# The first stage of an FFN, attention, FFN kernel: operands turned by DMA in place of TensorE

## The reference

```
x = x + 0.5 * ffn(layernorm(x))          # ffn: x and weight are quantised in blocks of 32 to a 6-bit grid
x = x + attention(layernorm(x))          #      with one scale a block, then xd @ wd.T + bias (512 x 512)
x = x + 0.5 * ffn(layernorm(x))

attention: qkv = x @ qkv_w.T + qkv_b (512 -> 1536), 16 heads of 32, each token looks at
           13 neighbouring tokens (window shifted inward at the ends of a sequence),
           softmax(q*scale . k + relative bias) . v, then @ proj_w.T + proj_b
```

## Time and profile before

| | us |
|---|---|
| median of 3 runs | 3375.26 (3371.84 to 3376.33) |
| profiled execution, its own time | 3373.88 |
| its span in the trace | 3372.0 |
| TensorE busy | 3001.5 (89%) |
| DVE busy | 2306.3 (68%) |
| ACT busy | 1888.3 (56%) |
| POOL busy | 1911.1 (57%) |

### The profile page before, as it was taken

The page is one execution under the profiler, slowest core; times in us unless marked ns, Lnnn a source line. Parts: engine busy times, 40 slices in busy tenths (PEclk is TensorE's granted clock), DMA queues, the critical chain, the costliest instruction groups (busy, mean ns, idle before and its releaser), DMA issues. The chain is left out here.

```text
span 3372.0 us, 68516 instructions
## 1 busy us (share of the span) xinstructions
PE 3001.5 (89%) x24864; PEld 1829.5 (54%) x24864; DVE 2306.3 (68%) x3170; ACT 1888.3 (56%) x2323; POOL 1911.1 (57%) x1497
## 2 busy tenths in 40 slices
PE   0399999999999999999978999999999999499999
PEld 0244444444444444444447877777777776244444
DVE  7467666666666766666556666666666665799995
ACT  2355555555555555556545666665666666566662
POOL 3354554554455455445326666666666665788883
PEclk9699999999999999999978999999999999699999
DMA  2123233323323323332247767677767674344442
GB/s 76 63 88 113 88 113 113 107 93 115 119 92 113 113 94 106 113 113 95 93 127 187 191 189 191 189 185 194 188 181 194 187 192 117 115 151 149 149 148 86
DMA packets 339610, 449.44 MB, mean 133 GB/s; under 512 B 23048, under 2 KB 254496, under 8 KB 331168
## 3 DMA queue, kind: packets, MB, share of 16 engines
q1 hardware_dynamic: 339360, 445.57, 43.4%
HBM read 243.85 MB, written 201.38 MB: 132 GB/s over the span
## 5 line engine op out<-in xcount | busy, mean ns | idle before, releaser
L761 DVE TENSOR_TENSOR fq_out_lo<-fq_val,fq_out_hi 128x512 f16<-128x512 f32 x384 | 460.7, 1237 | 289.8 <-ACT fq_out_hi L829 289.8
L946 PE MATMUL fq_acc<-fq_y_hi_t,w_qkv 128*128 128x512 f16 x2048 | 614.6, 379 | 1.6 <-ACT fq_y_hi_t L842 1.6
L1186 ACT ACTIVATE att_ctx<-att_o_ps 32x512 f32<-32x512 f32 x512 | 300.9, 588 | 365.0 <-PE att_o_ps L1295 358.7
L829 ACT CAST fq_out_hi<-fq_val 128x512 f16<-128x512 f32 x384 | 237.3, 618 | 319.1 <-DVE fq_val L758 311.0
L1270 PE MATMUL att_s_ps<-att_k,att_q_bd 128*128 128x44 f16 x6144 | 388.4, 217 | 26.2 <-DMA att_q_bd<-q_parts 16.9
L1270 PEld LDWEIGHTS att_s_ps<-att_k,att_q_bd 128*128 128x128 f16 x6144 | 382.1, 170 | 27.0 <-issue 26.0
L946 PE MATMUL fq_acc<-fq_y_lo_t,w_qkv 128*128 128x512 f16 x1024 | 388.5, 379 | 0.0
L946 PEld LDWEIGHTS fq_acc<-fq_y_hi_t,w_qkv 128*128 128x128 f16 x2048 | 200.1, 98 | 243.6 <-ACT fq_y_hi_t L842 1.8
L946 PE MATMUL fq_acc<-w_qkv,fq_y_hi_t 128*128 128x512 f16 x1024 | 304.9, 380 | 16.7 <-ACT fq_val L824 16.7
L966 PE MATMUL fq_acc<-w_ffn,fq_f_hi_t 128*128 128x512 f16 x1024 | 310.7, 386 | 1.4 <-DVE fq_f_lo_t L806 1.4
L632 PE MATMUL ffn_acc<-w_ffn,ffn_hi_t 128*128 128x512 f16 x1024 | 306.8, 381 | 4.5 <-DVE ffn_x_ring L518 4.4
(11 more groups left out here) (188 smaller groups left out, 6510.2 us busy)
## 6 DMA issues: line engine op xcount, KB each, us to landing
att_v<-v_parts SPq DMA_DIRECT2D x96, 704.0 KB
att_k<-k_parts SPq DMA_DIRECT2D x64, 524.0 KB, 7.1
fq_x<-in_L_attn_x SPq DMA_DIRECT2D x32, 1024.0 KB, 6.8
x_after_ffn<-fq_x SPq DMA_DIRECT2D x32, 1024.0 KB, 4.3
att_q_bd<-q_parts SPq DMA_DIRECT2D x512, 64.0 KB, 3.8
att_x<-x_after_ffn SPq DMA_DIRECT2D x32, 1024.0 KB, 5.9
x_after_attention<-att_x SPq DMA_DIRECT2D x32, 1024.0 KB, 9.2
ffn_x_ring<-x_after_attention SPq DMA_DIRECT2D x32, 1024.0 KB, 6.3
```

The lines of the kernel that those rows point to most:

```text
L761: dve.tensor_tensor(out=out[1][:, b], in0=val[:, b % RING], in1=out[0][:, b], op=ALU.subtract).then_inc(s["out_lo"], 1)
L829: act.copy(out[0][:, b], val[:, b % RING]).then_inc(s["out_hi"], 1)
L946: op = pe.matmul(acc[:, b % RING], w, m, start=(kc == 0 and (a, c) == (0, 0)), stop=(kc == KC - 1 and (a, c) == PARTS[-1]))
L1186: return act.activation(ctx_f[rows, u.u % 2].rearrange("p g (c q) -> p g c q", q=CHUNK), o_ps[rows, :, :, h, :], ACT.Copy, scale=1.0 / P_UP)
```

## The change

The 64 transposes that TensorE made for each group and the four copies out of PSUM are taken out. In their place SP issues four DMAs for each group (`dma_start_transpose`), from SBUF to SBUF, which write f_hi, f_lo, y_hi and y_lo transposed into `hi_t`, `lo_t`, `y_hi_t` and `y_lo_t`. Each names a source of 128x2048 fp16 and a destination of 128 x 16 x 128. `y_hi_t` and `y_lo_t` are doubled. `acc` now has all eight PSUM banks; the FFN uses banks 0 to 3, and block b of q, k and v uses bank (b + 4) % 8.

A group is now spread over four steps: t loads and takes statistics, q = t-1 is quantised, f = t-2 has its FFN and second norm, g = t-3 its q, k and v. The load of x is issued one step ahead, the store of v one step later. POOL computes the statistics of the first norm at the end of the step before the one that uses them. On DVE the value of the next v block is read before the lo part of the one at hand.

```diff
-    MID = NB - 2
+    BANKS = 8
...
-        hi, lo, hi_t, lo_t = (sb(n, [P, W], F16) for n in ("f_hi", "f_lo", "f_hi_t", "f_lo_t"))
-        y_hi, y_lo, y_hi_t, y_lo_t = (sb(n, [P, W], F16) for n in ("y_hi", "y_lo", "y_hi_t", "y_lo_t"))
+        hi, lo, y_hi, y_lo = (sb(n, [P, W], F16) for n in ("f_hi", "f_lo", "y_hi", "y_lo"))
+        hi_t, lo_t = (sb(n, [P, SUB, KC, P], F16) for n in ("f_hi_t", "f_lo_t"))
+        y_hi_t, y_lo_t = (sb(n, [P, 2, SUB, KC, P], F16) for n in ("y_hi_t", "y_lo_t"))
...
-        t_hi = ctx.enter_context(nc.psum_tensor("fq_t_hi", [P, KC, GROUP], F16))
-        t_lo = ctx.enter_context(nc.psum_tensor("fq_t_lo", [P, KC, GROUP], F16))
-        acc = ctx.enter_context(nc.psum_tensor("fq_acc", [P, RING, C], F32))
+        acc = ctx.enter_context(nc.psum_tensor("fq_acc", [P, BANKS, C], F32))
...
+                def turn_f(u):
+                    if u.within(GROUPS):
+                        need(sp, s["hi_done"], u.n + 1)
+                        take(sp, s)
+                        need(sp, s["ffn_done"], u.n * SUB)
+                        take(sp, s)
+                        sp.dma_start_transpose(hi_t[:].rearrange("p i g n -> p (i g) n"), hi[:]).then_inc(
+                            s["hi_turned"], 16)
+                        need(sp, s["lo_done"], u.n + 1)
+                        take(sp, s)
+                        sp.dma_start_transpose(lo_t[:].rearrange("p i g n -> p (i g) n"), lo[:]).then_inc(
+                            s["lo_turned"], 16)
...
+                def body(t):
+                    store_v(t.back(4))
+                    load(t.back(-1))
+                    store_x(t.back(2))
+                    turn_f(t.back(1))
+                    turn_y(t.back(2))
+                    store_q(t.back(3))
+                    store_k(t.back(3))
...
                 def body(t):
-                    f, g = t.back(1), t.back(2)
+                    q, f, g = t.back(1), t.back(2), t.back(3)
+                    if f.within(GROUPS):
+                        need(dve, s["x_biased"], f.n + 1)
+                        add_ffn(f, 0)
+                    if q.within(GROUPS):
+                        block_scales(q)
...
+                def ffn(u):
+                    need(pe, s["hi_turned"], 16 * (u.n + 1))
+                    need(pe, s["lo_turned"], 16 * (u.n + 1))
+                    for i in range(SUB):
+                        need(pe, s["qk_val"], (u.n - 2) * ACT_BLOCKS + KC + i + 1)
+                        need(pe, s["summed"], (u.n - 1) * SUB + i + 1)
...
                 def qkv(u, b):
                     n = u.back(-1)
-                    if b >= RING:
-                        need(pe, s["qk_val"], u.n * ACT_BLOCKS + b - RING + 1)
+                    if b < KC:
+                        need(pe, s["v_val"], (u.n - 1) * SUB + b + 1)
+                    elif b >= ACT_BLOCKS:
+                        need(pe, s["qk_val"], u.n * ACT_BLOCKS + b - ACT_BLOCKS + 1)
                     elif n.within(GROUPS):
-                        need(pe, s["summed"], n.n * SUB + b + 1)
+                        need(pe, s["summed"], n.n * SUB + b - KC + 1)
...
                 def body(t):
-                    f, g = t.back(1), t.back(2)
+                    f, g = t.back(2), t.back(3)
+                    if f.within(GROUPS):
+                        ffn(f)
                     if g.within(GROUPS):
...
+                        need(pe, s["y_hi_turned"], 16 * (g.n + 1))
+                        need(pe, s["y_lo_turned"], 16 * (g.n + 1))
+                        for b in range(NB):
                             qkv(g, b)
```

More of the change, by code:

```diff
@@ L687, in ffn_qkv_phase, with run, bank @@
         blocks = lambda t: t.rearrange("p (b c) -> p b c", c=BLOCK)
-        flat = lambda t: t.rearrange("p s c -> p (s c)")
-        channels_first = lambda t: t[:].rearrange("p (g n) -> p g n", g=KC)
         bw = [P, BLOCKS, BLOCK]
-        def run(eng, body):
-            steps(eng, U, 1, GROUPS // U, GROUPS + 3, body)
+        def run(eng, body, ahead=0):
+            steps(eng, U, 1, GROUPS // U - ahead, GROUPS + 4, body)
+        def bank(b):
+            return (b + KC) % BANKS
         def place_free(eng, u, b):
@@ L764, in body @@
                 def body(t):
-                    f, g = t.back(1), t.back(2)
+                    q, f, g = t.back(1), t.back(2), t.back(3)
[5 more added lines that the diff above has]
+                    if f.within(GROUPS):
+                        for i in range(1, SUB):
+                            add_ffn(f, i)
+                        need(dve, s["summed"], SUB * (f.n + 1))
+                        statistics(f, bst_y, mv_y, "y_stats", "y_averaged")
+                    if q.within(GROUPS):
+                        need(dve, s["rounded"], q.n + 1)
+                        need(dve, s["lo_done"], q.n)
+                        take(dve, s)
+                        dve.tensor_tensor(out=blocks(xd[:]), in0=blocks(q8[:]),
+                                          in1=scale_up[:, q.u % 2].unsqueeze(2).to_broadcast(bw),
+                                          op=ALU.mult).then_inc(s["dequantised"], 1)
                     if g.within(GROUPS):
-                        need(dve, s["y_turned_lo"], g.n + 1)
-                        need(dve, s["multiplied"], g.n * NB)
-                        dve.tensor_copy(channels_first(y_lo_t), t_lo[:]).then_inc(s["y_lo_out"], 1)
+                        for b in range(3):
+                            lo_of_block(g, b)
                     if t.within(GROUPS):
@@ L772, in body @@
                         statistics(t, bst, mv, "stats", "averaged")
[L773 to L786, removed]
-                        need(dve, s["floored"], t.n + 1)
-                        dve.tensor_scalar(scale_up[:, p], scale[:, p], LN_UP * FP8_UP, None, ALU.mult)
-                        dve.reciprocal(rscale[:, p], scale[:, p]).then_inc(s["scales"], 1)
@@ L790, in body @@
-                    if f.within(GROUPS):
-                        need(dve, s["summed"], SUB * (f.n + 1))
-                        statistics(f, bst_y, mv_y, "y_stats", "y_averaged")
-                    if t.within(GROUPS):
-                        need(dve, s["rounded"], t.n + 1)
-                        need(dve, s["lo_done"], t.n)
-                        take(dve, s)
-                        dve.tensor_tensor(out=blocks(xd[:]), in0=blocks(q8[:]),
-                                          in1=scale_up[:, t.u % 2].unsqueeze(2).to_broadcast(bw),
-                                          op=ALU.mult).then_inc(s["dequantised"], 1)
@@ L809, in body @@
+                        for b in range(ACT_BLOCKS, NB):
+                            if b + 1 < NB:
+                                v_value(g, b + 1)
                             lo_of_block(g, b)
```

201 lines of the change are left out of this document (93 added, 108 removed).

## The result

The changed kernel takes 3141.4 us (median of 4 runs, 3129.4 to 3145.8) against 3373.9 us before (median of 4 runs beside it, 3371.8 to 3376.3): a ratio of 0.9305, 95% interval 0.9278 to 0.9332. It is 7% faster; 3130 was forecast. The profiled execution has a span of 3141.4 us, 230.6 less than before's.

What follows compares the result with a forecast made beforehand. TensorE with its bank hand-offs was taken as the bound. From 3373.9 us, the last matmul 248.6 us earlier gives 3125.3; plus 1.4 for the median and 3 for unseen waits, 3130 us, range 3112 to 3475.

Steps and rivals of the forecast that it cites:

- TensorE's sum: First stage: without transposes and waits, TensorE's step is 192 matmuls, 41.44 us in place of 49.09, 7.65 us less.
- Fill and end: First stage's start and end: FFN 1 starts near 167 us, last matmul ends at 1484.7 in place of 1733.3.
- the 2.66 and 1.08 us: TensorE's idle time each step before the y transposes and before the first v block; both were to go.
- the ring through DVE, POOL and ACT: Not in the prediction for the kernel before: in-order engines waiting on each other in the first stage, 49.46 us a turn.
- rival 2: Part of the gain, through DMA time or another engine's order: step between 41.4 and 49.1 us, 3242 at 45; chance 0.14.
- Price of the transposes: Each of four added DMA transposes takes 2.4 us of the 16 DMA engines and 4.3 us from issue to data.
- Rivals 1 and 1b: DMA transposes in short runs, 9.2 us each: 3475 us, chance 0.12; or block by block, 30.4 us each: 5694, 0.12.
- The limit of D = 6.5 us: Time per DMA transpose at which the DMA engines become the bound: 4D + 15.4 = 41.4 us a step.
- Cover: f_lo and y_lo are each ready 16 us before their transposes are wanted, against 4.3 us to land.
- Copies off ACT and DVE: Two PSUM copies go from each engine per step, leaving ACT at 24.4 and DVE at 30.4 of 41.4 us.
- The worst case for DVE, 46.8 us: If all twelve out_lo subtractions ran at 2.37 us beside POOL, DVE would need 46.8 us a step and be the bound.
- What follows the stage: v's evacuation, stores and attention start as much earlier as the last matmul, 248.6 us, and are otherwise untouched.

Runs made afterwards that it cites:

- e12: Kernel before, with only ACT's and DVE's copies of f's transposes moved ahead of blocks 8 and 9: 3378.0 us, ratio 0.9986.
- e1: Changed kernel with the first stage's accumulators in four banks again instead of eight: 3153.4 us, ratio 0.9343.
- e14: Kernel before with the early copies, plus x's load and first-norm statistics one step ahead; TensorE still transposes, four banks: 3252.2 us, ratio 0.9629.
- e5: Changed kernel with SP's transposes held back until all twelve q, k and v blocks of the step are done: 3437.1 us, ratio 1.0172.
- e9: Kernel before, unedited, profiled a second time on another chip: 3374.6 us, ratio 0.9999.
- e7: Changed kernel with the attention's loop over 16 units in place of 8 on all engines but SP: 3115.0 us, ratio 0.9221.
- e8: Kernel before with the attention's loop over 16 units in place of 8 on all engines but SP: 3355.5 us, ratio 0.9938.
- e2: Changed kernel with 64 transposes a group put back on TensorE as dead work: 3266.5 us, ratio 0.9669.

## Why the prediction was right

*TensorE's sum.* Right: 192 matmuls at 0.216 us and nothing between them, 41.44 us from FFN to FFN as forecast. Fill and end came within 1 us of the forecast times.

*Why the waits go.* This step had the right number for the wrong reason, and that was luck. The prediction had "TensorE with its bank hand-offs sets the step" and took the 2.66 and 1.08 us for waits that fewer users and eight banks would remove. e12 removed the first and won nothing; e1 took the eight banks away and lost 0.36 us a step. What set the step was the ring through DVE, POOL and ACT, at 49.47 us. What broke it was the statistics' move to the step before (e14), which the change held and the prediction valued only as cover for the transposes; it named a loop through DVE, ACT and POOL only as a danger after the change (rival 2). The stage end went from 1732.9 to 1599.4 with the ring broken and the copies moved, 133.5 us, and by a further 114.6 us to 1484.8 when the transposes left TensorE. A kernel with DMA transposes and eight banks but the old order was not run.

*The clock.* The prediction compared step lengths at 1.00. Before's 200 to 1400 us had 0.98, since after every other wait a few matmuls ran at 1.2 GHz. One step before that of the earlier trace rows, the y transposes behind the wait read:

```profile
961.02 1.71 PE L925 MATMUL fq_t_hi<-ident,fq_y_hi 128*128 128x128 f16 x16 [3.04 <-ACT fq_f_hi_t L876]
962.53 1.91 PE L925 MATMUL fq_t_lo<-ident,fq_y_lo 128*128 128x128 f16 x16
```

1.91 us for what takes 1.06 at the full clock. From this wait to the one of the earlier trace rows it is 49.47 us (961.02 to 1010.49), one turn of the ring, with the slow matmuls inside: at full speed TensorE would only have waited longer. The new step was summed from its own 192 matmuls and not taken off the old one, so the forecast missed nothing here.

*Price of the transposes.* 4.2 to 4.8 us to land (4.3), 2.8 us of engine time (2.4), in pieces of 256 B. Rivals 1 and 1b fell. The Trainium skill's 1309 ns for a 128x128 block, in "VectorE: DVE Perf Modes", section "The three transpose paths", is no rate: 16 blocks landed in 4.2 to 4.8 us, at most 0.3 us each. SP is held 7.9 us a step by the four, not 1.6, inside the 16 us that the prediction allowed. The limit of D = 6.5 us, taken from packet time as a sum, was too strict: twelve transposes needed 45.7 us a step, not 48.7.

*Cover.* 16.3 us for f as forecast, 22 for y where 16 were forecast. e5 shows what it is worth: without it the kernel is 1.7% slower than before.

*Copies off ACT and DVE.* ACT 24.5 us a step (24.4), DVE 28.1 (30.4): `out_lo` takes 1044 ns on average where it took 1237, since fewer of them run beside POOL's long operations. Off TensorE's path after the change. The worst case for DVE, 46.8 us, has a slip: it takes off 12.0 us for the subtractions there are, which is eight of the twelve; the four of the v blocks took 0.69 us each, so it should be 44.1 us. Rival 2 leaned on it; it did not come up.

*What follows the stage.* Here the one miss in size: the attention was taken as untouched and cost 15.2 us more. The time is spent at the lower clock after idle stretches that were there before. e9 shows that the kernel before varies by 10 us in this by itself; the gap between the two groups of profiles, some 9 us, stays open. 3125.3 us forecast for the profiled execution, plus 0.5 for the stage's end, 15.2 and 2.3 behind it, is 3143.3; it took 3143.2.

## What to carry to other kernels

When a wait of the busiest engine is removed and its step stays as long, look for a ring through the in-order engines: find the longest idle stretch on each and what it waits for, see whether the same instruction comes back after exactly one step without the busiest engine in between, and move the start of that chain to the step before. A DMA transpose took work off TensorE at no cost here, as long as its data was ready a landing time and its queue's issues (7 us for a pair) before it was used; give it that cover first. Short idle stretches of TensorE can cost more than their length (18.2 us fewer of them gave 26 us in e7, 19.7 fewer gave 21 in e8), so a loop's turn is worth unrolling.

## What the runs showed of the hardware

- A DMA transpose of 128x2048 fp16 from SBUF to SBUF lands in 4.2 to 4.8 us, in packets of 256 B, and holds SP 1.3 us alone and 2.2 to 2.8 us behind another; eight in 41.5 us hide fully, twelve don't.
- TensorE loses about 3 us at each turn of the attention's loop (40.0 us in 13), and 8 of 13 such stretches in one profile were followed by a fall to 1.2 GHz, 2 of 13 in another of the same code.
- 64 transposes of 128x128 between matmuls cost 3.57 us, in eight pieces (e2) as in four (e14); in e2 about 0.4 us a step came on top, most of it where the loop turns.
- One of the four executions with eight DMA transposes a group took 12910 us; it was not the profiled one, and what held it is open.
